# A transformer layer's attention phase: sums in PSUM, an own bank for the output projection, paired splits of the probabilities

## What is computed

```python
x = L0_attn_h                                             # 8 x 1024 x 512, f32
x = x + layernorm(attn(layernorm(x)))                     # 16 heads of 32, causal
x = x + layernorm(ffn(layernorm(x)))                      # 512 -> 2048 -> 512
...
q, v, k = (qvk[:, :, 0], qvk[:, :, 1], qvk[:, :, 2])
scores = (einsum('bshi,bthi->bsth', q, k) + mask) / math.sqrt(d)
weights = softmax(scores, axis=2)
return einsum('bsth,bthi->bshi', weights, v).reshape(b, s, d) @ Wo
```

## Time and profile before

| | us |
|---|---|
| median of 3 runs | 3631.97 |
| lowest, highest | 3630.35, 3638.47 |
| the profiled execution | 3645.58 |
| its span in the profile | 3643.8 |
| attention in it | about 572 to 2189 |

### The profile page before, as it was taken

How to read it: one execution, slowest core, us unless ns; L and a number is a source line. 1 busy time by engine, 2 the same in 40 slices (tenths; PEclk the granted TensorE clock), 3 DMA queues, 4 the chain that set the end, 5 groups by cost and what they waited for, 6 DMA issues and landing times. The chain is left out here.

```text
span 3643.8 us, 69980 instructions
## 1 busy us (share of the span) xinstructions
PE 3210.2 (88%) x25389; PEld 1800.5 (49%) x25389; DVE 2468.9 (68%) x4477; ACT 2125.5 (58%) x2708; POOL 1468.3 (40%) x1087
## 2 busy tenths in 40 slices
PE   6999996888888887888888773999999999999998
PEld 2444442655555565656555541444444444444443
DVE  5444445988878787878788846566666666666665
ACT  2222221977878797969787873445454455445544
POOL 0000001988888898989898880000000000000000
PEclk9999996988898989999999986999999999999999
DMA  3334433122221312222222213001100000000000
GB/s 128 124 120 139 133 108 95 48 60 73 60 74 44 95 49 79 65 64 67 66 66 72 67 36 124 1 24 35 36 24 24 24 24 24 24 24 24 24 24 24
DMA packets 183089, 219.95 MB, mean 60 GB/s; under 512 B 15184, under 2 KB 129936, under 8 KB 182288
## 3 DMA queue, kind: packets, MB, share of 16 engines
q1 hardware_dynamic: 182800, 215.83, 19.0%
HBM read 130.84 MB, written 84.41 MB: 59 GB/s over the span
## 5 line engine op out<-in xcount | busy, mean ns | idle before, releaser
L929 POOL TENSOR_TENSOR a_prob_lo<-a_prob,a_prob_hi 128x1024 f16<-128x1024 f32 (+1 forms) x640 | 1237.7, 1958 | 203.4 <-ACT a_prob_hi L821 202.5
L849 DVE TENSOR_REDUCE a_mx<-a_pw 128x1 f32<-128x512 f32 (+3 forms) x1216 | 755.2, 657 | 142.0 <-PE a_pw L707 102.1
L814 ACT ACTIVATE a_prob<-a_pst,a_lift,a_exp_scale 128x1024 f32<-128x1024 f32 (+1 forms) x640 | 717.0, 1120 | 192.3 <-PE a_pst L756 97.8
L1376 PE MATMUL f_py<-f_w,f_act 128*128 128x512 f16 x3072 | 707.2, 380 | 22.1 <-DVE f_work L1142 12.8
L1366 PE MATMUL f_ph<-f_xT,f_w 128*128 128x512 f16 x3072 | 706.0, 380 | 0.4 <-issue 0.4
L821 ACT ACTIVATE a_prob_hi<-a_prob 128x1024 f16<-128x1024 f32 (+1 forms) x640 | 622.4, 973 | 0.0
L702 PE MATMUL a_pw<-a_kp,a_qp 96*128 96x512 f16 (+3 forms) x1536 | 499.5, 362 | 138.1 <-DVE a_mx L849 101.3
L1097 POOL TENSOR_TENSOR f_ve<-f_mv,f_eps 128x4 f32<-128x4 f32 x32 | 9.0, 282 | 1384.9 <-DVE f_mv L1123 1384.9
L751 PE MATMUL a_pst<-a_qp,a_kp 98*128 98x256 f16 (+1 forms) x2560 | 497.3, 279 | 78.6 <-ACT a_prob L814 55.8
L1314 ACT ACTIVATE f_hidden_work<-f_ph,f_turn,f_fold 128x512 f32<-128x512 f32 x256 | 199.0, 777 | 597.2 <-PE f_ph L1366 596.0
L1376 PEld LDWEIGHTS f_py<-f_w,f_act 128*128 128x128 f16 x3072 | 298.6, 98 | 379.8 <-issue 21.8
(11 more groups left out here) (174 smaller groups left out, 3934.7 us busy)
## 6 DMA issues: line engine op xcount, KB each, us to landing
qk_parts<-q_stage SPq DMA_DIRECT2D x128, 256.0 KB, 2.1
a_qp<-qk_parts SPq DMA_DIRECT2D x192, 128.0 KB, 2.6
a_kp<-qk_parts SPq DMA_DIRECT2D x192, 128.0 KB, 2.8
v_parts<-q_vstage SPq DMA_DIRECT2D x16, 1056.0 KB, 5.1
a_vt<-v_parts SPq DMA_DIRECT2D x32, 528.0 KB, 4.1
q_x<-in_L_attn_h_dram SPq DMA_DIRECT2D x16, 1024.0 KB, 7.7
a_xr<-in_L_attn_h_dram SPq DMA_DIRECT2D x64, 256.0 KB, 3.2
x<-a_y SPq DMA_DIRECT2D x64, 256.0 KB, 2.1
```

The costliest lines, as they stand in the source:

```text
L814: act.activation(prob[:, k % PR, :, off:QC], pst[:, k % 2, :, off:QC], ACT.Exp, scale=exp_scale[:, :], bias=lift[:, :]).then_inc(exp_done, 1)
L849: dve.tensor_reduce(out, src, AX_X, ALU.max).then_inc(released, 1)
L929: pool.tensor_tensor(prob_lo[:, k % HR, :, off:QC], prob[:, k % PR, :, off:QC], prob_hi[:, k % HR, :, off:QC], ALU.subtract).then_inc(lo_d ...
L1376: last = pe.matmul(py[:, t, :], act_r[:, f % AR, b, t * P:(t + 1) * P], w2s[:, a, f, :], start=(f == 0 and j == 0), stop=(f == NF - 1 and ...
```

## The change

- `acc` becomes one bank for both query tiles. The 66-column matmul becomes two of 33 columns that add into the same 33 columns as the low part's, so the sum is made in PSUM. `sums` and `osum` go; `normalise` reads PSUM, once TensorE has finished the chunk, and TensorE waits for it (`o_done`) before the next chunk.
- The maxima of both halves are written side by side and joined in one reduction from one SBUF tile.
- The output projection has a bank of its own, `pwo`, is no longer an item of the shared work, and waits until the tile before has been written (`y_done`). There is no copy: ACT turns `xr` into mean/sigma − x at slot s + 1 (`shift_x`), and DVE forms y·scale minus that (`wo_out`) ahead of its items of slot s + 2. `wo_add` and the fourth small operation go. The store comes at slot s + 3.
- Off the diagonal `high` and `low` take two steps at once, when the second is there. The ring of `prob` is 10 deep.
- `WO_AT_LAST` is changed.

```diff
-WO_AT_LAST = [10, 12, 14, 16, 19, 21, 28, 30]
-WO_SMALL, WO_NORM, WO_ADD, WO_STORE = 1, 2, 3, 4
+WO_AT_LAST = [10, 13, 16, 19, 22, 25, 28, 31]
+WO_SMALL, WO_NORM, WO_OUT, WO_STORE = 1, 1, 2, 3
...
-    PR, HR, YR = 5, 10, 4
+    PR, HR, YR = 10, 10, 4
...
-        acc = ps("acc", [P, TQ, CH])
+        acc = ps("acc", [P, CH])
+        pwo = ps("pwo", [P, D])
...
+            def halves_at(k):
+
+                c, j = STEPS[k]
+                if j >= TQ * c:
+                    return 1
+                return 2 * (j % 2)
...
+                def project(i, before, b, t, stage):
+                    n = QT * (i + b) + t
+                    wait(pe, y_done, n)
...
-                    if j == 0:
-                        wait(pe, acc_read, TQ * (NC * v + c - 1) + t + 1)
+                    if j == 0 and t == 0:
+                        wait(pe, o_done, NC * v + c)
                     for h in range(HPG):
-                        for part, skip in ((prob_hi, 0), (prob_lo, VF)):
...
+                        for part, low in ((prob_hi, 0), (prob_hi, VF), (prob_lo, 0)):
+                            col = h * VH + low
...
-                def wo_norm(i, t):
-                    act.wait_ge(small_done, 4 * (QT * i + t) + 4)
-                    act.activation(y[:, t % YR, :], y[:, t % YR, :], ACT.Identity, bias=small[:, t % YR, 3:4],
-                                   scale=small[:, t % YR, 1:2]).then_inc(y_norm, 1)
+                def shift_x(i, t):
+                    act.wait_ge(small_done, 3 * (QT * i + t) + 3)
+                    act.wait_ge(xr_loaded[t % 2], 16 * (QT // 2 * i + t // 2 + 1))
+                    act.activation(xr[:, t % 2, :], xr[:, t % 2, :], ACT.Identity, bias=small[:, t % YR, 2:3],
+                                   scale=-1.0).then_inc(x_shifted, 1)
...
-                            dve.tensor_tensor(mx[:, :, TPC:QT], mx[:, :, TPC:QT], mx2[:, :, :], ALU.max
-                                              ).then_inc(max_ready, 1)
+                            dve.tensor_reduce(mx[:, :, TPC:QT], mx2[:, :, :, :], AX_X, ALU.max).then_inc(max_ready, 1)
...
-                    dve.tensor_reduce(osum[:, t], acc[:, t, 0:HPG * VH].rearrange("p (h a f) -> p h f a", a=VP, f=VF),
-                                      AX_X, ALU.add).then_inc(acc_read, 1)
...
+                def wo_out(i, t):
+                    s, n = t % YR, QT * i + t
+                    dve.wait_ge(x_shifted, n + 1)
+                    wait(dve, y_stored[s], 16 * (QT // YR * i + t // YR))
+                    dve.scalar_tensor_tensor(y[:, s, :], pwo[:, :], small[:, s, 1:2], xr[:, t % 2, :], ALU.mult,
+                                             ALU.subtract
+                                             ).then_inc(y_done, 1)
...
                     for u, k in stage.slots:
+                        for b, t in stage.tiles(u, k, WO_OUT):
+                            wo_out(i + b, t)
...
-                def wo_add(i, t):
```

More of the change, by code:

```diff
@@ L354 @@
 NS = len(STEPS)
+SPLIT_OF = [sum(1 for cc, jj in STEPS[:k] if jj >= TQ * cc or jj % 2) for k in range(NS)]
+SPLITS = SPLIT_OF[-1] + 1
 LAST_OF_C = [max(k for k, (c, _j) in enumerate(STEPS) if c == cc) for cc in range(NC)]
@@ L426, in shared_work @@
                     out.append((u, k, "turn", e[0], c))
-            out += [(u, k, "wo", b, m) for b, m in self.tiles(u, k, 0)]
         return out
@@ L724, in shared @@
                                             ident[:, :])
-                    elif what == "turn":
+                    else:
                         pe.wait_ge(o_done, NC * (UNITS * i + unit) + m + 1)
@@ L728, in shared @@
                             last = pe.transpose(pw[:, bank, t * P:(t + 1) * P], o[:, m % 2, t, :], ident[:, :])
[L729 to L739, removed]
-                    last.then_inc(work_done, 1)
+                    last.then_inc(work_done, 1)
+                def project(i, before, b, t, stage):
+                    n = QT * (i + b) + t
+                    wait(pe, y_done, n)
+                    if t % TQ == 0:
+                        turn = next((n for n, it in enumerate(stage.work)
+                                     if it[2:] == ("turn", UNITS * b + UNITS - 1, t // TQ)), -1)
+                        pe.wait_ge(released, before + turn + 1)
+                    terms = [(g, a, w) for g in range(GROUPS) for w, a in PASSES]
+                    for j, (g, a, w) in enumerate(terms):
+                        last = pe.matmul(pwo[:, :], oT[:, a, g, t * P:(t + 1) * P], wo[:, w, g, :], start=(j == 0),
+                                         stop=(j == len(terms) - 1))
+                    last.then_inc(wo_done, 1)
                 def scores(i, u, k, heads):
@@ L802, in run @@
                                 shared(i, at, before, what, unit, m, stage)
+                        for b, t in stage.tiles(u, k, 0):
+                            project(i, before, b, t, stage)
                 for at, (what, m) in enumerate(AHEAD):
@@ L901, in shared @@
                         turned(i, unit, m, at, before, bank)
-                    elif what == "wo":
-                        wo_stats(i + unit, m, at, before, bank)
                     else:
@@ L912, in run @@
                         e = stage.earlier(u, k, LAG)
[L913 to L918 removed]
+                        if e and e[1] in LAST_OF_C:
+                            normalise(i, e[0], STEPS[e[1]][0])
+                        for b, t in stage.tiles(u, k, 0):
+                            wo_stats(i + b, t)
                 for at, (what, m) in enumerate(AHEAD):
@@ L958, in run @@
                             wo_small(i + b, t)
-                        for b, t in stage.tiles(u, k, WO_ADD):
-                            wo_add(i + b, t)
                 run_all(pool, run)
```

88 lines of the change are left out of this document (37 added, 51 removed).

## The result

The changed kernel takes 3766.8 us (median of 4 runs, 3756.4 to 3770.5), the kernel before 3633.6 (4 runs): a ratio of 1.036, interval 1.034 to 1.039. It is slower by 133 us, as forecast in sign; the forecast was 3721. The profiled execution took 3756.4, span 3754.4, against 3645.6 and 3643.8, so the two traces differ by 110.6 us. That of the changed kernel is the lowest of its series, that of the kernel before lies above its median, which is why the medians are further apart.

What follows compares the result with a forecast made beforehand. The prediction took an ACT and POOL loop to bound the heavy stretch of attention; +127 heavy, −52 light, −4 start and +18 tail gave +89 us on 3632, so 3721 us, range 3600 to 3810.

Steps and rivals of the forecast that it cites:

- Heavy part: Seven intervals per batch border with an output-projection tile every four steps: +18.2 us each, seven times, +127 us.
- the 97.7 of the count: Heavy part counted interval by interval over ACT, POOL and TensorE's delay, before the clock term: 97.7 us against 83.0, +14.7.
- the 90 with TensorE never late: Lower bound of the heavy part, if TensorE never delays the scores: about 90 us.
- the faster rival: Small numbers ready when ACT asks, heavy intervals 2.1 us shorter: −157 us, 3475; chance 0.13.
- scores(10) at 5.1: Step 6 to 10: TensorE, held up by maxima behind `wo_out`, delivers step 10's scores 5.1 us after the shift starts.
- The clock after TensorE's stop: Heavy part: TensorE at 1.2 GHz after stops lengthens the path by 0 to 10.5 us a batch; 3.5 taken.
- Light part: The 52 steps between heavy parts: 112 us falls to 105, −7.4 each, seven times, −52 us.
- POOL's stalls: Light part: two VectorE operations get in POOL's way; of 10 us lost to this and TensorE's clock, the stalls go.
- 127 us for 4608 more matmuls: Splitting the 66-column product costs TensorE 127 us, 4.0 a unit, covered while the clock holds.
- The tail: Last batch, step 10 to the last tile start: 41.9 us becomes 60.2, four tiles in series; +18, bounds +14 and +20.
- The start of attention: The first batch's units without tiles, before the first tile instruction: −4 us.
- the milder faster case: Heavy part merely stays at 83.0: −38 us, 3594; part of the waits-vanish rival, chance 0.13 for the whole.

Runs made afterwards that it cites:

- out_behind: The changed kernel with `wo_out` behind the maxima of its VectorE slot instead of ahead of them: 3696.1 us, 1.021 of the kernel before.
- no_pairs: The changed kernel with `high` and `low` one step at a time again, the shift left where the change put it: 3816.7 us, 1.054 of the kernel before.
- b_mx: The kernel before with only the maxima of both halves joined in one reduction: 3610.1 us, ratio 0.996.
- b_psum: The kernel before with only the sums of probabilities times values made in PSUM (three 33-column matmuls): 3623.7 us, ratio 0.998.
- b_pairs: The kernel before with only `high` and `low` off the diagonal taken two steps at a time and the `prob` ring 10 deep: 3807.2 us, ratio 1.050.
- b_all_but_bank: The kernel before with pairs, PSUM sums and joined maxima, without the projection's own bank, its slots and its tail list: 3548.4 us, ratio 0.978.
- shift_later: The changed kernel with ACT's shift one slot later, `wo_out` and the store moved with it: 3741.5 us, 1.033 of the kernel before.

## Why the prediction was right, and where it was off

- **Heavy part**, +18.2 each: measured +18.3. The mechanism has its rows: shifts 17.8 us apart, POOL idle 3.81 us behind the small numbers, the stop of TensorE. It was the sum of the ACT and POOL count and of TensorE's delay. out_behind, with about a quarter of TensorE's waits for the maxima gone, gives 94.2, between the 97.7 of the count and the 90 with TensorE never late; half of the difference from 97.7 is in the interval 18 to 2, 11.8 for 13.5. Removing the shift's place as well gives 84.9.
- **What held it.** I wrote that the order "puts a pair of lows, 4.06, ahead of the small steps" and hung the case against the faster rival on that. The rows have the pair there (6.14 us of lows ahead of the small numbers), but it is not what alone holds the loop: no_pairs was slower. The round from the shift through `wo_out`, the maxima, TensorE, the projection and exp(11) back to POOL is about as long. In the prediction TensorE's round stood as a term in the sum, scores(10) at 5.1; as a bound of its own it was not counted.
- **The clock after TensorE's stop**: I took 3.5 us a batch, up to 10.5. In the stretch shown scores(10) came at 7.5 and not 5.1, at a clock of 0.50, which makes that interval 17.8 instead of 15.3. The prediction had stops of some 5 us in every interval; from 10 to 14 they are 4.7 and 5.2 in the mean, from 14 to 18 about 3.3, from 6 to 10 only 1.8, and from 2 to 6 none is over 1. Against the count, 6 to 10 is 2.0 over and the two intervals from 10 to 14 are 1.2 over each, 14 to 18 and 2 to 6 are as counted (15.4, 15.5 and 12.1), and 18 to 2 is 1.2 under it: net 3.6, the 3.5 that I took as a guess between 0 and 10.5. That this fits so closely is luck.
- **Light part**: −7.4 forecast, −5.0 measured, times seven 17 us too much. The pairs cost what was forecast, 4.07 us on POOL (4.06) and a pitch of 1.82 on ACT (1.81). VectorE's two operations fell from 1248 to 424 and from 1261 to 186 ns; groups by form of the kernel after:

```profile
L882 DVE TENSOR_TENSOR a_o<-a_acc,a_rden 128x256 f32<-128x256 f32 x115 | 48.8, 424 | 4.0
...
L866 DVE TENSOR_REDUCE a_mx<-a_mx 128x16 f32<-128x32 f32 x30 | 5.6, 186 | 1.0
```

- I priced that fall at POOL's stalls and otherwise at nothing, "all beside busier ACT and POOL". As a sum this holds for the kernel before (b_mx and b_psum give 0.4 and 0.2%); as a reason it misses that the pairs would not work without it. b_pairs shows it: 5.0% for an edit that I priced, alone, as a saving.
- **TensorE**: 127 us for 4608 more matmuls was too high. Timeline of TensorE after, the first and the last rows of twelve matmuls of L787, and what follows them:

```profile
1463.23 0.20 PE L787 MATMUL a_acc<-a_vt,a_prob_hi 128*128 128x33 f16 x2
...
1463.50 0.18 PE L787 MATMUL a_acc<-a_vt,a_prob_lo 128*128 128x33 f16 x1
1463.53 0.38 PE L760 MATMUL a_pst<-a_qp,a_kp 98*128 98x256 f16 x2
```

  Twelve starts in 0.30 us are 25.0 ns each, not 27.5: three narrow ones 75, where a wide and a narrow one took some 57 (seven pitches in 0.20 us), so 18 ns × 4608 = 83 us. *The Trainium skill's floor of about 25 ns, in "TensorE: Matmul & The Clock Gate", Wait — 56ns, not 53.3ns?, was nearer than my reading of a row that mixed both widths.* It was covered, as said.
- **The tail**: +18 forecast, bounds 14 and 20; measured +28, outside them. The four tiles in series take 6.5 to 9.9 us each, not 6.4: 8.6, 6.5, 9.9, 8.0; the first interval 14.7, not 12.7. The term that was mis-sized is the projection, 2.6 in the sum. Its twelve matmuls take 4.85, 2.76, 5.28 and 4.26 us in these four, after stops of TensorE of 4.91, 2.27, 4.43 and 3.77 us; the second and the third:

```profile
2276.60 2.76 PE L747 MATMUL a_pwo<-a_wo,a_oT 128*128 128x512 f16 x12 [2.27 <-DVE a_y L906]
```

```profile
2284.01 5.28 PE L747 MATMUL a_pwo<-a_wo,a_oT 128*128 128x512 f16 x12 [4.43 <-DVE a_oT L891]
```

  The granted clock was 1.00 in the one (2.4 GHz) and 0.50 in the other (1.2 GHz). The prediction gave the clock after a stop a price in the heavy part and none in the tail. The longer projections are some 6 of the 7.4 us by which the four tiles exceed 25.6.

The first and the last tile instruction of the tail in the kernel after:

```profile
2229.72 0.72 ACT L839 ACTIVATE a_xr<-a_xr,a_small 128x512 f32<-128x512 f32 x1 [4.29 <-POOL a_small L955]
...
2299.53 0.72 ACT L839 ACTIVATE a_xr<-a_xr,a_small 128x512 f32<-128x512 f32 x1 [7.31 <-POOL a_small L955]
```

- **The start of attention** to the first tile: −4 forecast, −9.5 measured.
- **The total**: 3721 forecast, 3767 measured, 133 us more than before instead of 89. The terms above explain 22 of the missing 44 (light +17, tail +10, start −5.5); by the other 22 the medians lie further apart than the two profiled executions. Two slips don't bear on this: the upper bounds add up to +191, not +189, and the range's lower end, 3600, does not take in the milder faster case, 3594.
- **The faster rival** ("waits vanish with the work") asked for small numbers ready in time. b_all_but_bank is what it describes, without the own bank: heavy 79.0, light 103.7. It needed the slots of the kernel before.

## What to carry to other kernels

An instruction that waits for another engine belongs behind the work that nobody should wait for, not at the head of its queue: one `wo_out` of 0.75 us ahead of two maxima cost 1.5%, and a shift one step earlier 2.6% once that was out of the way. Where two rounds through the engines are about equally long, an edit that shortens one of them shows nothing or a loss (shift_later, no_pairs); the shift's place had its price only once `wo_out` stood behind the maxima. A stage that leaves TensorE waiting can pay a second time, by a lower clock in the work that follows, and in a tail too. And a joined instruction on GpSimd is only as cheap as what VectorE does beside it: count the VectorE operations with two operands in SBUF before making GpSimd's instructions longer.

## What the runs showed of the hardware

- A VectorE operation with two SBUF operands that starts while a GpSimd low is running ends with that low: the normalisation 0.3 us after it in 119 of 119 cases of the kernel before (1248 ns in the mean, lows of 2.1 us) and 89 of 89 of b_pairs (2404 ns, lows of 4.07), the join at its end in 30 of 30 and 29 of 29. In b_psum only 15 of 31 joins did; the other 16 ended two lows later (4.2 us), which makes the mean 3043 ns. What decides between these I can't say.

```profile
L849 DVE TENSOR_TENSOR a_mx<-a_mx 128x16 f32<-128x16 f32 x32 | 97.4, 3043 | 1.1
```

- Matmuls of 33 columns, each with its own weights, follow each other every 25.0 ns at the 2.4 GHz level.
- After a stop of 1.79 us TensorE's next 6.1 us ran at a granted clock of 0.50; in the tail a stop of 2.27 us was followed by 2.6 us at 1.00, and one of 4.43 us by 4.9 us at 0.50.
